# Mamba block and mixture of experts on one Trainium2 core: the step-size product on VectorE, one more buffer for the rows of B and of C, and fewer small tiles

## The chip, the cores and the metric

The kernel runs on one core of one Trainium2 chip. The metric is the device time of one execution in microseconds (us). The engines are called as in the profile: PE is TensorE (PEld its weight loads), DVE is VectorE, ACT is ScalarE, POOL is GpSimd, SP is SyncE, whose queue issues most DMAs.

## The reference

Sixteen rows (batch entries) of 512 tokens with 256 features pass through two stages. `mod` are six vectors for each row, made from `L0_c` and `L0_wmod`. In short:

```python
h = layernorm(x) * (1 + ca) + sa
x = x + ga * mamba(h)              # ga, gb: absolute value at least 0.25
h = layernorm(x) * (1 + cb) + sb
x = x + gb * experts(h)

def mamba(h):
    xb, z = split(norm(h) @ W_in)          # 512 channels each
    xb = silu(conv3(xb) + conv_b)
    dt = softplus(xb @ W_dt + b_dt)
    B, C = xb @ W_B, xb @ W_C              # 16 states
    for t in tokens:                       # A = -exp(A_log), for 512 channels and 16 states
        state = exp(dt[t] * A) * state + (dt[t] * xb[t]) * B[t]
        y[t] = sum_over_states(state * C[t])
    return h + ((y + D * xb) * silu(z)) @ W_out

def experts(h):                            # 16 experts, width 128, the best 4 of 2 groups out of 4
    return sum_e weight[t, e] * (silu(h @ gate[e]) * (h @ up[e])) @ down[e]
```

All of it is computed in float32.

## The kernel before

Everything of one row lives in SBUF with channels on the 128 partitions and the 512 tokens along them: `xb`, `gz` (the gate), `dt` and `dtx` have four blocks of 128 channels each, [128, 4, 512].

**The scan.** The work is cut into 512 steps `g`: 16 rows (a row has one slot of 32 steps), and in a row two pairs of channel blocks, each with 16 states. The states are walked up in one pair and down in the next, so that the rows of B and C used last in one pair are used first in the next. One step `g` takes, on [128, 2, 512] = 128x1024 elements:

- ACT, `decay` (L1112): two exponentials into a PSUM bank pair, `hbank[g % 2]`;
- POOL, `drive(g)` (L1335): `unit[g % 5] = dtx * B row`, run AHEAD = 2 steps before its use;
- DVE, `scan(g)` (L759): the recurrence as one tensor_tensor_scan in the PSUM bank;
- DVE, `times_c(g)` (L773): the states times the row of C, back into `unit` (the first two of a pair into `gsum`);
- POOL, `add(g - 1)` (L1347): a DMA that adds the 512 KB of `unit` to `gsum[k]`, k being g's parity; each waits until the last one of its parity has landed.

The rows of B and C are read from DRAM, broadcast over the partitions (256 KB each), by SP's queue: `load_b(g + B_LEAD)` and `load_c(g + C_LEAD)` in step g, into B_RING and C_RING buffers. `rows_held` works out which loads can be left out since the row is still in its buffer. Before, B has four buffers and a lead of 3, C three and a lead of 2.

**Step sizes.** `dtx = dt * xb` for a pair of blocks must stand before that pair's first `drive`. Before, `step_sizes` on POOL makes it (L1278: one 128x1024 product; then L1280, a memset of the two first columns of `dt` to 1e30, which cuts the scan between the two blocks). This happens 31 times; the very first product is made on DVE (`first_steps`, L837, L839).

**Beside the scan**, each engine runs the same fixed list of other stages, `streams(slot, ...)`: a stage is a generator, and its steps are spread over the moments of a slot (three to a step g; part 0, 1 and 2). ACT runs one moment behind PE, DVE two, POOL and SP three. So `step_sizes1` (second pair of the slot's row, moments 1 to 8) did its product on POOL in moment 11, step 3 of the slot, behind `drive(g + 2)`; `step_sizes0` (first pair of the coming row, moments 73 to 80) in moment 83, step 27, again behind `drive(g + 2)`.

**The experts** of the row before run at the same time, in 16 half-steps of two experts. For each: PE makes gates and ups (L504) into two of three `wbank`s; ACT the tanh of the gates into one tile, `etanh` (L1102); DVE silu (L730, `act = (etanh + 1) * gates`) and the product with the ups (L737); POOL the product with the routing weights (L1302); PE the down product (L516) into `mbank`. After the first and the second eight, DVE scales `mbank` and adds it to the result (L747, L750), and PE's next down product waits for that. `act` has two buffers.

Every engine runs its instructions in order, so one that waits holds all that stand behind it.

Of the kernel before, what the change touches and what calls it, by code (L numbers as in the profile page):

```python
# [10 lines left out]
P = 128  # L11
# [71 lines left out]
def build(nc, d, out):  # L83
# [15 lines left out]
    B_RING, C_RING, W_RING = 4, 3, 2  # L99
    B_LEAD, C_LEAD = 3, 2  # L100
# [17 lines left out]
    with ctx:  # L118
# [15 lines left out]
        half_ident = sb("half_ident", [P, P])  # L134
# [32 lines left out]
        etanh = sb("etanh", [P, 2 * HT])  # L167
        w_all = sb("w_all", [P, W_RING, 2, HT])

        sums = sb("sums", [P, TT])  # L170
        squares = sb("squares", [P, TT])
        nmean = sb("nmean", [P, TT])
        ve = sb("ve", [P, TT])
        rstd = sb("rstd", [P, TT])
        shift = sb("shift", [P, TT])
        sums2 = sb("sums2", [P, TT])
        squares2 = sb("squares2", [P, TT])
        nmean2 = sb("nmean2", [P, TT])
        ve2 = sb("ve2", [P, TT])
        rstd2 = sb("rstd2", [P, TT])  # L180
        shift2 = sb("shift2", [P, TT])
        r_th = sb("r_th", [P, TT, E])
# [6 lines left out]
        r_cut = sb("r_cut", [P, TT, E + 4])  # L189
# [3 lines left out]
        w_tok = sb("w_tok", [P, TT, E])  # L193
# [170 lines left out]
        def _(eng):  # L364
# [158 lines left out]
            def mix(row, pair):  # L523

                p = 2 * row + pair
                for a in range(2):
                    q = 2 * pair + a
                    t = fill(("y", row, q))
                    eng.matmul(t.bank[:, :], diag_d[:, q, :], xb[:, xb_at(row, q), :], start=True, stop=False)  # L529
                    for k in range(2):  # L530
                        need.wait_ge(summed[k], 16 * LATER * (p + 1))
                        m = eng.matmul(t.bank[:, :], half_ident[:, :], gsum[:, (2 * p + k) % SUMS, a, :], start=False,  # L532
                                       stop=k == 1)
                    m.then_inc(t.full, 1)
                    yield
                    yield
# [77 lines left out]
        def _(eng):  # L614
# [21 lines left out]

            def gates(row):
                for q in range(DK):
                    t = work.at["gate", row, q]
                    need.wait_ge(gate_act, DK * row + q + 1)  # L640
                    eng.scalar_tensor_tensor(out=gz[:, q, :], in0=gz[:, q, :], scalar=1.0, in1=t.bank[:, :],  # L641
                                             op0=ALU.add, op1=ALU.mult).then_inc(t.free, 1)
                    yield
                    yield

            def pick(row):
# [4 lines left out]
                bias = choice_bias[:, :].rearrange("p (a e) -> p a e", a=1).to_broadcast([P, TT, E])  # L651
                need.wait_ge(route_act, 2 * row + 2)
# [69 lines left out]
            def experts(row):  # L722
                for s in range(E + 1):
                    n = E * row + s
                    a = act[:, n % MOE_RING, :, :].rearrange("p j t -> p (j t)")
                    if s < E:

                        t = work.at["gates2", row, s]
                        need.wait_ge(etanhed, n + 1)
                        eng.scalar_tensor_tensor(out=a, in0=etanh[:, :], scalar=1.0, in1=t.bank[:, :], op0=ALU.add,  # L730
                                                 op1=ALU.mult).then_inc(t.free, 1)
# [151 lines left out]
            for m_ in range(DK):  # L883
                eng.tensor_scalar(diag_d[:, m_, :], ident[:, :], d_par[:, m_:m_ + 1], 0.5, ALU.mult,
                                  ALU.mult).then_inc(scaled_w, 1)
            eng.tensor_scalar(half_ident[:, :], ident[:, :], 0.5, None, ALU.mult).then_inc(scaled_w, 1)

            turning = turn_chunks()
            for _ in range(2 * EARLY):
                next(turning)  # L890
            stage_of = {"silu_first": lambda r: silu_inputs(r, 0),
                        "silu_last": lambda r: silu_inputs(r, 1), "gates": gates,
                        "mix0": lambda r: mix(r, 0), "mix1": lambda r: mix(r, 1),
# [26 lines left out]
        def _(eng):  # L920
# [101 lines left out]
            def gates(row):  # L1022
                for q in range(DK):
# [5 lines left out]
                    eng.activation(gz[:, q, :], t.bank[:, :], ACT.Tanh, scale=0.5).then_inc(gate_act, 1)  # L1029
# [64 lines left out]
            def experts(row):  # L1094
                for s in range(E + 1):
                    if s < E:
                        t = work.at["gates2", row, s]
                        need.wait_ge(t.full, t.after)
                        if E * row + s:
                            used = work.at["gates2", *divmod(E * row + s - 1, E)]  # L1100
                            need.wait_ge(used.free, used.after)
                        eng.activation(etanh[:, :], t.bank[:, :], ACT.Tanh, scale=0.5).then_inc(etanhed, 1)  # L1102
# [111 lines left out]
        def _(eng):  # L1214
# [54 lines left out]
            def step_sizes(row, q):  # L1269
                pair = slice(2 * q, 2 * q + 2)  # L1270
                for _ in range(8):
                    yield
                for m_ in (2 * q, 2 * q + 1):
                    t = work.at["dt", row, m_]
                    need.wait_ge(t.free, t.after)
                xb_ready(need, row)
                x0 = xb_at(row, 2 * q)
                eng.tensor_tensor(dtx[:, pair, :], dt[:, pair, :], xb[:, x0:x0 + 2, :], ALU.mult).then_inc(dtx_made, 1)  # L1278
                need.wait_ge(dtx_made, 2 * row + q + 1)
                eng.memset(dt[:, pair, 0:1], FAR).then_inc(dt_cut, 1)  # L1280
                yield

# [55 lines left out]
            def add(g):  # L1338
# [6 lines left out]
                if u >= 4:  # L1345
# [18 lines left out]
            stage_of = {"norms": norms, "step_sizes0": lambda r: step_sizes(r, 0),  # L1364
                        "step_sizes1": lambda r: step_sizes(r, 1), "stats": stats, "scale_wo": scale_wo,
                        "scale_h": scale_h}
# [232 lines left out]
```

## Time and profile before

| | before |
|---|---|
| median of 3 runs | 2733.24 us (2730.16 to 2736.14) |
| the profiled execution: its time, its span | 2725.84 us, 2724.1 us |
| granted TensorE clock, mean | 0.949 |
| PE busy | 2363.2 us, 87% |
| DVE busy | 2402.8 us, 88% |
| ACT busy | 1452.3 us, 53% |
| POOL busy | 2227.2 us, 82% |
| DMA: moved, mean rate | 596.53 MB, 219 GB/s |
| chain of work that ended last | PE 51%, POOL 14%, DVE 10%, DMA 9%, issue 9%, ACT 6% |

The profile comes from one execution that is 7.4 us quicker than the median. Busy shares are means over the span, which has a start of some 65 us without a scan and an end of some 130 us with experts alone; between them one slot follows another in about 158 us. The profile shows an instruction from its dispatch to its end, so neighbours on one engine may overlap by some tenths of a microsecond. The number in brackets behind a row of the order of time is the idle time in front of it, with what ended it; where the named releaser had long been done, it was another, often a DMA.

### The profile page before, as it was taken

How to read it: one execution, taken by the hardware profiler on the slowest of the kernel's cores; microseconds unless marked ns; L12 is line 12 of the kernel's file. 1: busy time of each engine (PE TensorE's matmuls, PEld its weight loads, DVE VectorE, ACT ScalarE, POOL GpSimd, SP SyncE). 2: the span in 40 equal slices, each digit the busy share in tenths (PEclk: the TensorE clock that was granted, in tenths of full speed). 3: DMA queues.
4: the chain of work that ended last, by engine and by line, in shares of the span. 5: the costliest groups of instructions: out<-in, count | busy, mean ns of one | idle time of the engine just before them, and what ended most of it. 6: DMA issues, size and time to landing. Idle time of an engine off the chain costs nothing.

```text
span 2724.1 us, 28747 instructions
## 1 busy us (share of the span) xinstructions
PE 2363.2 (87%) x9006; PEld 1679.9 (62%) x9006; DVE 2402.8 (88%) x2395; ACT 1452.3 (53%) x2760; POOL 2227.2 (82%) x1559
## 2 busy tenths in 40 slices
PE   6454998989999898998989899998989989898799
PEld 2222675666667566666656666675666657566678
DVE  4798999999999999999899999999999899999922
ACT  4455646565554656565465655546565554654311
POOL 2588899888889989888898888889888889987922
PEclk8676998999999999999999999999999999999999
DMA  5989898999989899999989899898989999898921
GB/s 136 248 200 247 201 251 218 241 218 234 242 218 251 216 243 222 237 239 222 238 217 235 218 233 242 213 246 221 245 215 233 239 216 247 221 234 212 247 55 51
DMA packets 338235, 596.53 MB, mean 219 GB/s; under 512 B 49680, under 2 KB 160272, under 8 KB 338080
## 3 DMA queue, kind: packets, MB, share of 16 engines
q0 software_dynamic: 72960, 243.30, 46.7%
q1 hardware_dynamic: 265120, 351.38, 41.6%
q8 instruction: 71, 1.16, 0.2%
q14 instruction: 84, 0.69, 0.1%
HBM read 349.62 MB, written 10.06 MB: 132 GB/s over the span
## 4 chain that ended last, share of the span: by engine, by line
PE 51%; POOL 14%; DVE 10%; DMA 9%; issue 9%; ACT 6%; SPq 0%; POOLq 0%; DVEq 0%; ACTq 0%
PE wbank L504 17%; PE mbank L516 9%; PE wbank L406 7%; POOL unit L1335 6%; DVE hbank L759 5%; DMA gsum<-unit 4%; PE wbank L446 4%; PE wbank L532 3%; PE wbank L394 3%; POOL act L1302 2%; POOL gsum L1347 2%; PE wbank L417 2%; PE wbank L529 2%; DMA w_all<-w_scratch 2%; ACT z L939 2%
## 5 line engine op out<-in xcount | busy, mean ns | idle before, releaser
L1335 POOL TENSOR_TENSOR unit<-dtx,b_bc 128x1024 f32<-128x1024 f32 x512 | 1353.3, 2654 | 40.7 <-DVE dtx L837 28.1
L759 DVE TENSOR_TENSOR_SCAN hbank<-hbank,unit 128x1024 f32<-128x1024 f32 x512 | 1173.1, 2291 | 83.3 <-ACT hbank L1112 78.8
L1112 ACT ACTIVATE hbank<-dt,a_neg 128x512 f32<-128x512 f32 x1024 | 668.0, 681 | 262.9 <-DVE unit L773 230.7
L516 PE MATMUL mbank<-down_t,act 128*128 128x256 f32 x2048 | 522.8, 393 | 70.9 <-POOL act L1302 50.3
L773 DVE TENSOR_TENSOR unit<-hbank,c_bc 128x1024 f32<-128x1024 f32 x448 | 546.4, 1220 | 26.1 <-DMA c_bc<-bc_scratch 2.5
L1347 POOL DMA_DIRECT2D gsum<-unit x448 | 449.3, 1003 | 126.8 <-DMA gsum<-unit 63.4
L1302 POOL TENSOR_TENSOR act<-act,w_all 128x512 f32<-128x512 f32 x256 | 363.2, 1419 | 212.1 <-DVE act L737 190.3
L504 PE MATMUL wbank<-h_t,up_t 128*128 128x256 f32 x2048 | 501.1, 389 | 10.3 <-DVE gz L641 10.3
L516 PEld LDWEIGHTS mbank<-down_t,act 128*128 128x128 f32 x2048 | 394.9, 196 | 175.7 <-POOL act L1302 69.1
L504 PE MATMUL wbank<-h_t,gate_t 128*128 128x256 f32 x2048 | 485.7, 380 | 0.0
L504 PEld LDWEIGHTS wbank<-h_t,up_t 128*128 128x128 f32 x2048 | 395.1, 195 | 107.6 <-DVE gz L641 28.8
L504 PEld LDWEIGHTS wbank<-h_t,gate_t 128*128 128x128 f32 x2048 | 386.7, 190 | 89.9 <-issue 39.0
L1102 ACT ACTIVATE etanh<-wbank 128x512 f32<-128x512 f32 x256 | 150.7, 589 | 319.5 <-PE wbank L504 319.3
L730 DVE SCALAR_TENSOR_TENSOR act<-etanh,wbank 128x512 f32<-128x512 f32 x256 | 173.9, 679 | 94.7 <-ACT etanh L1102 93.1
L406 PE MATMUL wbank<-xb,w_dt 128*128 128x512 f32 x496 | 233.1, 616 | 8.8 <-DVE xb L633 8.8
L737 DVE TENSOR_TENSOR act<-act,wbank 128x512 f32<-128x512 f32 x256 | 174.0, 680 | 18.8 <-PE wbank L504 13.5
L430 PE MATMUL wbank<-xn_t,w_in 128*128 128x512 f32 x256 | 143.1, 688 | 29.7 <-DVE gz L641 22.4
L406 PEld LDWEIGHTS wbank<-xb,w_dt 128*128 128x128 f32 x496 | 96.6, 198 | 111.8 <-issue 107.3
L532 PE MATMUL wbank<-gsum,half_ident 128*128 128x512 f32 x256 | 125.3, 610 | 27.2 <-DMA gsum<-unit 27.2
L394 PE MATMUL wbank<-xn_t,w_in 128*128 128x512 f32 x256 | 125.4, 615 | 26.4 <-DVE xb L633 22.2
L376 PE MATMUL wbank<-ident,z 128*128 128x128 f32 x256 | 42.2, 305 | 101.7 <-ACT z L939 95.1
L446 PE MATMUL wbank<-w_out,gz 128*128 128x256 f32 x512 | 121.1, 379 | 1.1 <-issue 1.1
(142 smaller groups left out, 2237.5 us busy)
## 6 DMA issues: line engine op xcount, KB each, us to landing
gsum<-unit POOLq DMA_DIRECT2D x448, 512.0 KB, 7.5
c_bc<-bc_scratch SPq DMA_DIRECT2D x464, 256.0 KB, 5.6
b_bc<-bc_scratch SPq DMA_DIRECT2D x448, 256.0 KB, 6.2
w_all<-w_scratch SPq DMA_DIRECT2D x256, 256.0 KB, 4.9
ht<-in_L_attn_x_dram SPq DMA_DIRECT2D x16, 512.0 KB, 5.2
w_out<-in_L_attn_W_out_dram SPq DMA_DIRECT2D x16, 512.0 KB, 6.4
ht<-in_L_attn_x_dram POOLq DMA_DIRECT2D x16, 512.0 KB, 8.5
out_dram<-xt SPq DMA_DIRECT2D x16, 512.0 KB, 3.3
```

The source lines that it names most:

```text
L394: m = eng.matmul(t.bank[:, :], w_in[:, k, q * P:(q + 1) * P], xn_t[:, k, :], start=k == 0, stop=k == HK - 1)
L406: m = eng.matmul(t.bank[:, :], w_dt[:, k, m_ * P:(m_ + 1) * P], xb[:, xb_at(row, k), :], start=k == 0, stop=k == DK - 1)
L446: m = eng.matmul(t.bank[:, u * H:(u + 1) * H], gz[:, k, c:c + P], w_out[:, k, :], start=k == 0, stop=False)
L504: m = eng.matmul(t.bank[:, j * HT:(j + 1) * HT], w[:, 2 * first + j, k, :], h2_t[:, row % 2, k, h * HT:(h + 1) * HT], start=k == 0, stop=k ...
L516: m = eng.matmul(mbank[:, u * H:(u + 1) * H], act[:, (n - 1) % MOE_RING, j, u * P:(u + 1) * P], down_t[:, e, :], start=(e == 0 and u == 0) ...
L532: m = eng.matmul(t.bank[:, :], half_ident[:, :], gsum[:, (2 * p + k) % SUMS, a, :], start=False, stop=k == 1)
L759: eng.tensor_tensor_scan(h, h, unit[:, g % RING, :, :].rearrange("p a t -> p (a t)"), 0.0, ALU.mult, ALU.add).then_inc(scanned, 1)
L773: eng.tensor_tensor(o, hbank[g % HB][:, :, :], c_bc[:, s:s + 1, :].to_broadcast([P, 2, T]), ALU.mult).then_inc(c_scaled, 1)
L1112: eng.activation(hbank[g % HB][:, a, :], dt[:, 2 * q + a, :], ACT.Exp, scale=a_neg[:, 2 * q + a, n:n + 1]).then_inc(decayed, 1)
L1302: eng.tensor_tensor(a, a, w_all[:, n % W_RING, :, :], ALU.mult).then_inc(weighted, 1)
L1335: eng.tensor_tensor(unit[:, g % RING, :, :], dtx[:, 2 * q:2 * q + 2, :], b_bc[:, s:s + 1, :].to_broadcast([P, 2, T]), ALU.mult).then_inc(d ...
L1347: eng.dma_start(gsum[:, (2 * p + k) % SUMS, :, :], unit[:, g % RING, :, :], accum_op=ALU.add).then_inc(summed[k], 16)
```

## The change

Five things are changed.

1. `step_sizes` moves from POOL's program to DVE's, at the same place of the plan. With DVE's lag it comes one moment earlier: `step_sizes1` in moment 10, behind `times_c` of step 3 and a product of `mix1`; `step_sizes0` in moment 82, between `times_c` of step 27 and the scan of step 28. It waits for `dt` (ACT) as before, and for the `drive`s of the row before.
2. B gets five buffers with a lead of 4, C four with a lead of 3.
3. ACT writes the experts' tanh into the `act` tile itself and DVE's silu works in place; ACT's wait for the silu before becomes a wait for the down product that last read that tile.
4. `half_ident` is gone. The factor 0.5 of the gate goes into the second half of `w_in`, scaled once at the start (a 128x1024 instruction on DVE in place of a 128x128 one).
5. Twelve statistics tiles become one, `r_cut` and `w_tok` share memory with `r_two` and `r_ch`; `pick` gets a wait for PE's last read of `w_tok`, a slot earlier.

```diff
-    B_RING, C_RING, W_RING = 4, 3, 2
-    B_LEAD, C_LEAD = 3, 2
+    B_RING, C_RING, W_RING = 5, 4, 2
+    B_LEAD, C_LEAD = 4, 3
...
-        half_ident = sb("half_ident", [P, P])
...
-        etanh = sb("etanh", [P, 2 * HT])
...
-        r_cut = sb("r_cut", [P, TT, E + 4])
+        r_cut = r_two[:, :, :].rearrange("p g k -> p (g k)")[:, 0:TT * (E + 4)].rearrange("p (t e) -> p t e", t=TT)
...
-        w_tok = sb("w_tok", [P, TT, E])
+        w_tok = r_ch
...  mix, on PE
-                        m = eng.matmul(t.bank[:, :], half_ident[:, :], gsum[:, (2 * p + k) % SUMS, a, :], start=False,
+                        m = eng.matmul(t.bank[:, :], ident[:, :], gsum[:, (2 * p + k) % SUMS, a, :], start=False,
...  on DVE
+            def step_sizes(row, q):
+                pair = slice(2 * q, 2 * q + 2)
+                for _ in range(8):
+                    yield
+                for m_ in (2 * q, 2 * q + 1):
+                    t = work.at["dt", row, m_]
+                    need.wait_ge(t.free, t.after)
+                if row:
+                    need.wait_ge(driven, (row - 1) * NU + (q + 1) * NS)
+                x0 = xb_at(row, 2 * q)
+                eng.tensor_tensor(dtx[:, pair, :], dt[:, pair, :], xb[:, x0:x0 + 2, :], ALU.mult).then_inc(dtx_made, 1)
+                need.wait_ge(dtx_made, 2 * row + q + 1)
+                eng.memset(dt[:, pair, 0:1], FAR).then_inc(dt_cut, 1)
+                yield
...  pick, on DVE
+                if row:
+                    w = work.at["w", row - 1]
+                    need.wait_ge(w.full, w.after)
...  experts, on DVE
-                        eng.scalar_tensor_tensor(out=a, in0=etanh[:, :], scalar=1.0, in1=t.bank[:, :], op0=ALU.add,
+                        eng.scalar_tensor_tensor(out=a, in0=a, scalar=1.0, in1=t.bank[:, :], op0=ALU.add,
...  at the start, on DVE
-                eng.tensor_scalar(diag_d[:, m_, :], ident[:, :], d_par[:, m_:m_ + 1], 0.5, ALU.mult,
+                eng.tensor_scalar(diag_d[:, m_, :], ident[:, :], d_par[:, m_:m_ + 1], None,
                                   ALU.mult).then_inc(scaled_w, 1)
-            eng.tensor_scalar(half_ident[:, :], ident[:, :], 0.5, None, ALU.mult).then_inc(scaled_w, 1)
+            eng.tensor_scalar(w_in[:, :, INNER:2 * INNER], w_in[:, :, INNER:2 * INNER], 0.5, None,
+                              ALU.mult).then_inc(scaled_w, 1)
...  gates, on ACT
-                    eng.activation(gz[:, q, :], t.bank[:, :], ACT.Tanh, scale=0.5).then_inc(gate_act, 1)
+                    eng.activation(gz[:, q, :], t.bank[:, :], ACT.Tanh).then_inc(gate_act, 1)
...  experts, on ACT
-                        t = work.at["gates2", row, s]
+                        n, t = E * row + s, work.at["gates2", row, s]
                         need.wait_ge(t.full, t.after)
-                        if E * row + s:
-                            used = work.at["gates2", *divmod(E * row + s - 1, E)]
-                            need.wait_ge(used.free, used.after)
-                        eng.activation(etanh[:, :], t.bank[:, :], ACT.Tanh, scale=0.5).then_inc(etanhed, 1)
+                        if n >= MOE_RING:
+                            need.wait_ge(down_done, n - MOE_RING + 1)
+                        eng.activation(act[:, n % MOE_RING, :, :].rearrange("p j t -> p (j t)"), t.bank[:, :], ACT.Tanh,
+                                       scale=0.5).then_inc(etanhed, 1)
...  on POOL
-            def step_sizes(row, q):
...
-                eng.tensor_tensor(dtx[:, pair, :], dt[:, pair, :], xb[:, x0:x0 + 2, :], ALU.mult).then_inc(dtx_made, 1)
...
-                eng.memset(dt[:, pair, 0:1], FAR).then_inc(dt_cut, 1)
```

## Rows read from the trace of the kernel before

**Rows 1.** Engines' busy times by stretch, one slot: PE, PEld, DVE, ACT, POOL, clock, DMA share, GB/s
```profile
1178.00:1336.00 158.00, 141.18 (x546) 99.59 (x545) 146.79 (x146) 88.01 (x168) 136.85 (x97) 0.98 0.92 229
```

**Rows 2.** Chain that ended last, in order of time, first slot: start, us, what
```profile
80.53 2.31 POOL dtx L1278
```

**Rows 3.** In order of time, POOL and DVE, slot 7: steps 27 and 28
```profile
1296.23 2.94 POOL L1335 TENSOR_TENSOR unit<-dtx,b_bc 128x1024 f32<-128x1024 f32 x1
1298.54 2.94 POOL L1278 TENSOR_TENSOR dtx<-dt,xb 128x1024 f32<-128x1024 f32 x1
...
1297.37 2.29 DVE L759 TENSOR_TENSOR_SCAN hbank<-hbank,unit 128x1024 f32<-128x1024 f32 x1
1300.15 0.69 DVE L730 SCALAR_TENSOR_TENSOR act<-etanh,wbank 128x512 f32<-128x512 f32 x1 [0.50 <-ACT etanh L1102]
```

**Rows 4.** Instructions of L837 and L710: ns min/median/max, first and last start
```profile
L837 DVE TENSOR_TENSOR dtx<-dt,xb x1: 1226/1226/1226, 52.9 to 52.9; 128x1024 f32<-128x1024 f32 x1
...
L710 DVE SCALAR_TENSOR_TENSOR r_w<-r_cut,r_s x16: 224/226/1749, 269.1 to 2623.6; 128x64 f32<-128x64 f32 x16
```

**Rows 5.** In order of time, POOL and DVE: L710 in slot 7, then the long one
```profile
1216.43 0.23 DVE L710 SCALAR_TENSOR_TENSOR r_w<-r_cut,r_s 128x64 f32<-128x64 f32 x1
...
1218.18 0.89 POOL L1347 DMA_DIRECT2D gsum<-unit  x1 [3.10 <-DMA gsum<-unit]
...
2491.89 3.03 POOL L1335 TENSOR_TENSOR unit<-dtx,b_bc 128x1024 f32<-128x1024 f32 x1
...
2493.27 1.75 DVE L710 SCALAR_TENSOR_TENSOR r_w<-r_cut,r_s 128x64 f32<-128x64 f32 x1
```

**Rows 6.** In order of time, DVE and POOL, slot 7: what hands work to PE
```profile
1306.75 0.69 DVE L750 TENSOR_TENSOR xt<-mbank,xt 128x512 f32<-128x512 f32 x1
1311.27 0.68 DVE L737 TENSOR_TENSOR act<-act,wbank 128x512 f32<-128x512 f32 x1
...
1287.96 1.26 POOL L1302 TENSOR_TENSOR act<-act,w_all 128x512 f32<-128x512 f32 x1 [0.43 <-DVE act L737]
```

**Rows 7.** In order of time, PE, its two pauses behind step 28, slot 7
```profile
1307.59 1.97 PE L516 MATMUL mbank<-down_t,act 128*128 128x256 f32 x8 [1.19 <-DVE xt L750]
...
1316.09 1.13 PE L516 MATMUL mbank<-down_t,act 128*128 128x256 f32 x4 [3.09 <-POOL act L1302]
1317.06 5.29 PE L406 MATMUL wbank<-xb,w_dt 128*128 128x512 f32 x8
...
1324.78 3.60 PE L406 MATMUL wbank<-xb,w_dt 128*128 128x512 f32 x8
```

**Rows 8.** The same, PE, slots 1 and 14, first and last of the 14
```profile
366.63 1.13 PE L516 MATMUL mbank<-down_t,act 128*128 128x256 f32 x4 [1.48 <-POOL act L1302]
...
2432.27 1.13 PE L516 MATMUL mbank<-down_t,act 128*128 128x256 f32 x4 [2.14 <-POOL act L1302]
2433.24 5.29 PE L406 MATMUL wbank<-xb,w_dt 128*128 128x512 f32 x8
```

**Rows 9.** Engines' busy times by stretch: PE, PEld, DVE, ACT, POOL, granted clock, DMA share
```profile
1318.00:1320.00 2.00, 2.00 (x3) 0.67 (x2) 1.90 (x3) 0.12 (x1) 1.24 (x1) 0.50 0.87 216
```

**Rows 10.** In order of time, POOL and DVE, slot 8: steps 3 and 4
```profile
1335.05 2.63 POOL L1335 TENSOR_TENSOR unit<-dtx,b_bc 128x1024 f32<-128x1024 f32 x1
...
1336.80 0.69 DVE L730 SCALAR_TENSOR_TENSOR act<-etanh,wbank 128x512 f32<-128x512 f32 x1 [0.71 <-ACT etanh L1102]
1338.06 2.30 DVE L759 TENSOR_TENSOR_SCAN hbank<-hbank,unit 128x1024 f32<-128x1024 f32 x1 [0.57 <-ACT hbank L1112]
```

**Rows 11.** Who waited for whom: us in total, times, longest us
```profile
POOL act L1302 <- DMA w_all<-w_scratch: 19.3, 9, 9.6
POOL unit L1335 <- DMA b_bc<-bc_scratch: 9.5, 7, 3.2
```

**Rows 12.** DMA issues: count, KB each, median us to landing
```profile
c_bc<-bc_scratch SPq DMA_DIRECT2D x464, 256.0 KB, 5.6
```

**Rows 13.** In order of time, DVE at the start: four 128x128 scalings
```profile
54.21 7.24 DVE L884 TENSOR_SCALAR diag_d<-ident,d_par 128x128 f32<-128x128 f32 x4
```

More of the change, by code:

```diff
@@ L166, in build @@
         act = sb("act", [P, MOE_RING, 2, HT])
-        etanh = sb("etanh", [P, 2 * HT])
         w_all = sb("w_all", [P, W_RING, 2, HT])
[L170 to L182, printed above, removed]
+        stat = sb("stat", [P, 12, TT])
+        sums, squares, nmean, ve, rstd, shift, sums2, squares2, nmean2, ve2, rstd2, shift2 = (
+            stat[:, k, :] for k in range(12))
         r_s = sb("r_s", [P, TT, E])
@@ L892, in _ @@
                         "silu_last": lambda r: silu_inputs(r, 1), "gates": gates,
+                        "step_sizes0": lambda r: step_sizes(r, 0), "step_sizes1": lambda r: step_sizes(r, 1),
                         "mix0": lambda r: mix(r, 0), "mix1": lambda r: mix(r, 1),
@@ L1267, in norms @@
                 yield
-            def step_sizes(row, q):
[L1270 to L1277, printed above, removed]
-                eng.tensor_tensor(dtx[:, pair, :], dt[:, pair, :], xb[:, x0:x0 + 2, :], ALU.mult).then_inc(dtx_made, 1)
-                need.wait_ge(dtx_made, 2 * row + q + 1)
-                eng.memset(dt[:, pair, 0:1], FAR).then_inc(dt_cut, 1)
-                yield
             def stats(row):
@@ L1362, in _ @@
             need.wait_ge(consts, 7)
-            stage_of = {"norms": norms, "step_sizes0": lambda r: step_sizes(r, 0),
-                        "step_sizes1": lambda r: step_sizes(r, 1), "stats": stats, "scale_wo": scale_wo,
-                        "scale_h": scale_h}
+            stage_of = {"norms": norms, "stats": stats, "scale_wo": scale_wo, "scale_h": scale_h}
             first_norm()
```

## The prediction

> **What bounds the kernel now.** I read the busy times of one slot first. Slots repeat every 158 us, and in one of them PE is busy 141 us, DVE 147, POOL 137, and the DMA engines 0.92 of the time [rows 1]. Nothing has much room, so the busy shares don't say who sets the time. The chain of waits does: it passes from engine to engine, and three questions matter. Where is POOL's product L1278 on it? Where would DVE's new instruction stand on it? Who is waiting just behind that place?
>
> L1278 itself stands on the chain once in 31 times, in the first slot [rows 2]. So its removal from POOL is worth little by itself.
>
> The new instruction has two places. The first is step 27, between `times_c(27)` and `scan(28)`. There DVE goes on at 1297.37 without a pause, has one pause of 0.50 us at 1300.15, in front of L730 [rows 3], and then none until L750 and L737, which end at 1307.44 and 1311.95 [rows 6]. Both are awaited by PE: after L750 by 0.15 us, with a pause of 1.19 us in front, and after L737 by way of POOL's L1302 (1.26 us), with a pause of 3.09 us [rows 6, 7]. Behind this PE goes from product to product. So from step 28 to step 31 the chain is DVE's, and all that is put ahead of it arrives at PE less 0.50 us. The second place is step 3: there DVE has pauses of 0.71 and 0.57 us right behind [rows 10], since ACT's tanh waits for PE. There PE sets the time.
>
> **Part 1: the product on DVE.** On DVE the same instruction took 1.226 us; the memset of two columns, with its wait for the product, lies between 0 and the 0.225 of L710 with its 64 elements [rows 4], and I put it at 0.10. That is 31 times 1.33, 41 us, if nothing else happens. But something else can happen: this instruction reads two SBUF tensors (`dt`, `xb`). Another DVE instruction that does so is L710. Fifteen of 16 took some 0.225 us; one took 1.75 [rows 4]. The fifteen ran while POOL ran no product, as the one of slot 7, in a pause of POOL of 3.10 us. The long one began at 2493.27, when a `drive` of POOL was running that ended at 2494.92, and it ended at 2495.02 [rows 5], 0.10 us behind. DVE waited until POOL had finished. The start shows the same with another kind of instruction: four scalings of 128x128 took 7.24 us together, beside three `drive`s [rows 13].
>
> So every L710 that met a product of POOL was held, but that is one. The Trainium skill, SBUF — State Buffer, section "SBUF: two separate sides", says that VectorE and GpSimd share a pair of ports as an exclusive lock, held for a whole instruction, and that a VectorE instruction with two SBUF inputs takes it against a GpSimd one that reads SBUF. Perfetto Trace Analysis (Optimizing Scalar/DVE Operations) warns for that reason that moving work between these two "might not help". By that rule the new product waits each time that it meets a `drive`, which makes the 3.0 us below; taken as an accident, the long L710 would leave 1.25 us there, and the sum would be that of the first rival.
>
> I take the blocking, since the one event agrees with it and none speaks against it.
>
> Then at step 27: a `drive` is running when DVE arrives at 1297.37; it ends at 1296.23 + 2.94 = 1299.17 [rows 3]. The product ends 1.226 - 0.225 + 0.10 = 1.10 us later, at 1300.27, and with the memset `scan(28)` starts at 1300.4, 3.0 us late. Less the pause of 0.50, everything up to L737 is 2.5 us late. It is so in each slot 1 to 14 (DVE and POOL stand to each other as here in all of them, to 0.2 us); slot 0 has no experts, slot 15 no product here.
>
> What arrives at PE: the first pause grows from 1.19 to 3.7 us. PE then comes to its second one at 1316.09 - 3.09 + 2.5 = 1315.5; L737 ends at 1314.45 and L1302 at 1315.7. So PE goes on some 0.25 us behind its arrival in place of G, the second pause of today: the shift of a slot is 2.75 - G. G is 1.48 in slot 1, 2.14 in slot 14 [rows 8], 3.09 in slot 7, and 1.8 in the mean of the 14, the shortest being 1.2. That gives 0.95 x 14 = +13 us. That G shrinks is POOL's gain: without L1278, which occupied it until 1301.48 [rows 3], its `add`s go out up to 2.3 us earlier and no longer hold L1302.
>
> **PE's clock.** Behind the pause of 3.09 us in slot 7 the granted clock was 0.50 for a stretch [rows 9], the lower level of 1.2 GHz, and the eight matmuls of L406 took 5.29 us in place of 3.60 [rows 7], 1.7 more. Behind 2.14 us in slot 14 it was the same [rows 8]. Three of the 14 slots show it here (7, 8, 14), the other eleven don't, with pauses of 1.2 to 2.4 us. A first pause of 3.7 us in each slot is longer than any of these, so I expect the low clock behind most of them: a slot with it shifts by 2.5 + 1.7 - G = 2.4, 34 us in all 14, less 5 for the three of today: +29. Between +13 (no new one) and +29 I take three quarters of the way, +25. Bounds: +8 (none, and today's three gone) to +29.
>
> **At step 3** a `drive` ends at 1337.68, so the product ends at 1338.78 and L730 starts at 1338.9 in place of 1336.80; the scan at 1338.06 is 1.4 us late after the two pauses. What hides it is PE, busy without a pause for the next 20 us, with ACT behind it. Taken at 0; if that cover is gone, 16 x 1.4 = +23 us. Below 0 it can't be: POOL's time there is no one's wait.
>
> **Part 2: buffers for B and C.** At the turn of a slot's two pairs the last rows of the first pair are reused: five and four in place of four and three. By `rows_held`, C's loads fall from 464 to 448 [rows 12] and B's by 16 too, so two of 256 KB less in a slot. And SP leaves them out just when it stores the routing weights and reads the first `w_all`, which L1302 awaits: 19.3 us in 9 waits, 9.6 of it one; the rows of B were awaited for 9.5 us [rows 11]. At best all but the 9.6 goes, -19; at worst nothing, as POOL or DVE are next at those places within 0.4 us in slot 7. Nothing speaks for a loss: a load still waits for the step before last's reader, and SP's queue is held no longer. I take -7.
>
> **Parts 3 to 5.** Nothing. ACT's tanh waits only for PE today, and PE's gates come behind the down product that frees the tile. The in-place silu has one SBUF input like before. The wait in `pick` was over a slot earlier. At the start, scaling half of `w_in` is the last instruction ahead of DVE's first turned weights: 0.4 us more than `half_ident`, or 2.4 if a `drive` blocks it as the ones before [rows 13]; against this stand up to 2.3 us that the chain of the first slot loses with L1278 [rows 2]. I take 0, with -2 to +2.
>
> **The sum:** +25 + 0 - 7 + 0 = +18 us: 2744 for the profiled execution of 2725.84, which was 7 us under the median, and 2733 + 18 = **2751 us** for the median.
>
> **Rivals.**
> - *Not held, and faster.* If the long L710 is an accident, or if the relieved POOL runs no `drive` when DVE arrives, DVE is late by 1.33 - 0.08 overlap - 0.50 = 0.75 us only, at the same place. PE's shift is 0.75 + 0.25 - G = -0.8, times 14 -11 us; the first pause stays under 2 us, the three low clocks go (-5), and the loads give -7: -23, 2710 us. It decides when DVE's delay is under G - 0.25, 1.5 us. For it: POOL loses 2.9 us of work at each place, so its schedule may move. Against it: the long L710 [rows 5], and that POOL has nothing new between steps 4 and 26 to move it. 0.22.
> - *Balance.* Blocked, but the clock stays high behind the longer pause (+8), and the loads give more (-8): about 2733 us. 0.17.
> - *DVE is late everywhere.* The delay of step 3 isn't hidden either: +18 + 23 = 2774 us. For it: DVE has but 11 us of pauses in a slot of 158 [rows 1]. Against it: PE's unbroken run there. 0.08. And in the extreme no pause takes up anything: 15 x 3.0 + 16 x 2.7 = 88 us, with the loads 2814 us. 0.07.
> - *The forecast*, 2739 to 2765 us: 0.46.
>
> **Range and chances.** 2706 to 2776 us leaves out the extreme and the lower half of the fast rival's spread. Both signs hold much of the chance; the likeliest case's own range is 2739 to 2765. A measurement of this kernel can tell some 0.2%, 5.5 us, from no change. Faster 0.24 (the first rival and a little of the balance), same 0.16 (the rest of it and an edge of the forecast), slower 0.60.
>
> **What would show it.** The new DVE product: about 2.9 us at step 27 and 2.7 at step 3 if held, 1.23 if not. PE's pause in front of L516 behind L750: 3.7 us against 1.9. The clock in the stretch behind it: 0.5 or 1. PE's second pause: short in both. The scan of step 28: 3.0 us behind `times_c(27)`. L1302's waits for `w_all`: shorter. The forecast is wrong if the product is short, or if PE's lateness at step 31 is made up by a pause later in the slot that I took for fixed.

## The result and the profile after

The changed kernel takes 2759.72 us (median of 4 runs, 2757.09 to 2765.98), the kernel before, beside it, 2731.7 (2726.53 to 2736.14): 1.0113 times the time, 95% interval 1.0089 to 1.0137. It is slower by 28 us between the medians (31 by the ratio), where 18 were forecast, and the time lies inside the range.

| | after |
|---|---|
| the profiled execution: its time, its span | 2761.49 us, 2759.8 us |
| granted TensorE clock, mean | 0.938 |
| DMA: moved, mean rate | 588.13 MB, 213 GB/s |

The profiled executions are 35.7 us apart: that of before was some 6 us under its median, that of after 2 us above. First the busy times, then the chain that ended last:

```profile
PE 2380.3 (86%) x9006; PEld 1698.5 (62%) x9006; DVE 2491.7 (90%) x2457; ACT 1452.2 (53%) x2760; POOL 2154.5 (78%) x1497
```

```profile
PE 34%; DVE 28%; issue 14%; POOL 13%; ACT 7%; DMA 4%; SPq 0%; DVEq 0%; POOLq 0%
```

DVE is 89 us busier, which is 31 times 2.87, and its share of the chain goes from 10 to 28%. POOL is 73 us less busy, though its product had been on the chain only once. Next the engines' busy times in one slot (PE, PEld, DVE, ACT, POOL, clock, DMA share, GB/s), which answers [rows 1]:

```profile
1208.00:1366.00 158.00, 142.62 (x547) 102.22 (x546) 151.05 (x151) 88.28 (x169) 132.50 (x93) 0.97 0.90 225
```

And the moved product by its durations (minimum, median, maximum in ns, first and last start):

```profile
L635 DVE TENSOR_TENSOR dtx<-dt,xb x31: 2751/2887/5065, 86.2 to 2489.3; 128x1024 f32<-128x1024 f32 x31
```

None of the 31 took the 1.226 us of its free form [rows 4]: each met a `drive` and ended 1.09 us behind the end of one. In order of time in slot 7, POOL and DVE, steps 27 and 28 (answers [rows 3]):

```profile
1327.35 2.93 POOL L1329 TENSOR_TENSOR unit<-dtx,b_bc 128x1024 f32<-128x1024 f32 x1
...
1328.48 2.89 DVE L635 TENSOR_TENSOR dtx<-dt,xb 128x1024 f32<-128x1024 f32 x1
1331.43 0.06 DVE L637 MEMSET dt<- 128x2 f32 x1
1331.48 2.30 DVE L765 TENSOR_TENSOR_SCAN hbank<-hbank,unit 128x1024 f32<-128x1024 f32 x1
```

The `drive` ends at 1330.28, the product at 1331.37, 1.09 us behind, and the scan starts 3.0 us after DVE could have started it. What PE gets of that (answers [rows 7]):

```profile
1341.10 2.73 PE L504 MATMUL mbank<-down_t,act 128*128 128x256 f32 x8 [3.59 <-DVE xt L756]
1343.62 2.85 PE L492 MATMUL wbank<-h_t,gate_t 128*128 128x256 f32 x8
1346.31 1.89 PE L492 MATMUL wbank<-h_t,up_t 128*128 128x256 f32 x8
1348.04 1.03 PE L504 MATMUL mbank<-down_t,act 128*128 128x256 f32 x4
1348.90 3.60 PE L394 MATMUL wbank<-xb,w_dt 128*128 128x512 f32 x8
```

The first pause is 3.6 us (1.19 before), the second is gone, and the eight down products and the eight gates behind the pause take 2.73 and 2.85 us against 1.97 and 1.89 at full clock. The granted clock there, in slots 1, 7 and 14 (columns as above):

```profile
376.20:379.20 3.00, 3.00 (x7) 2.45 (x8) 3.00 (x3) 0.00 (x0) 2.75 (x2) 0.50 1.05 254
...
1341.50:1344.50 3.00, 3.00 (x11) 2.39 (x10) 3.00 (x3) 0.00 (x0) 2.34 (x1) 0.61 0.99 252
...
2464.50:2467.50 3.00, 3.00 (x10) 2.47 (x9) 3.00 (x3) 0.00 (x0) 2.44 (x2) 0.61 1.05 271
```

In all of the slots 1 to 14 the clock is 0.50 to 0.68 in such a stretch. Before, it never fell behind the first pause, and behind the second one in three of the 14. The waits over the whole span (us in total, times, longest), the first two lines of before, then of after (POOL's two answer [rows 11]):

```profile
PE mbank L516 <- DVE xt L750: 20.6, 15, 3.9
...
PE mbank L516 <- POOL act L1302: 50.3, 35, 4.0
```

```profile
PE mbank L504 <- DVE xt L756: 51.7, 15, 3.6
...
PE mbank L504 <- POOL act L1296: 13.1, 12, 3.5
...
POOL act L1296 <- DMA w_all<-w_scratch: 9.4, 1, 9.4
POOL unit L1329 <- DMA b_bc<-bc_scratch: 0.2, 1, 0.2
```

PE waits 31 us more for DVE and 37 less for POOL, so the waits alone don't explain the loss. The whole account of steps 28 to 31, from the rows of slots 1 to 14, is this, in the mean of a slot: the first pause is 2.4 us longer and the second, 1.8 us, is gone; the products of PE between the first pause and the first of L394 (before, of L406) take 7.9 us in place of 6.4 at the lower clock; and the eight of L394 take 0.4 less than those of L406, since the three low stretches of before are gone. Together that is +1.7 us, 24 us in 14 slots.

**Where the time lies.** The starts of the 512 scans cut a span into parts: up to the first scan, slot 0, slots 1 to 14 in first halves (steps 0 to 15, with the place of step 3) and second halves (with that of step 27), slot 15 up to the end of its last scan, the end. What step 27 does can reach into steps 0 to 2 of the next slot, and so into a first half. In us, one profiled execution each:

| kernel | start | slot 0 | 1–14, first halves | 1–14, second halves | slot 15 | end |
|---|---|---|---|---|---|---|
| before | 64.9 | 149.5 | 1110.4 | 1108.3 | 151.0 | 140.0 |
| after | 69.4 | 156.9 | 1114.7 | 1131.6 | 147.1 | 140.0 |
| only_steps | 65.3 | 154.7 | 1108.6 | 1144.9 | 148.8 | 141.2 |
| rings_back | 63.9 | 155.5 | 1113.2 | 1144.4 | 149.1 | 139.9 |
| both_pool | 68.1 | 150.6 | 1112.1 | 1106.6 | 146.5 | 142.2 |
| first_pair_pool | 68.2 | 153.6 | 1113.0 | 1103.3 | 148.0 | 139.9 |
| second_pair_pool | 67.6 | 149.7 | 1111.8 | 1135.2 | 148.4 | 144.2 |
| ahead_sbuf | 66.3 | 153.4 | 1124.9 | 1157.1 | 146.6 | 142.0 |
| ahead_psum | 67.0 | 149.3 | 1088.9 | 1113.5 | 146.0 | 140.0 |
| early_scalings | 59.5 | 154.3 | 1112.3 | 1130.0 | 146.9 | 142.7 |
| both_pool_early | 60.9 | 148.9 | 1113.1 | 1103.8 | 147.6 | 141.3 |
| dt_from_psum | 60.4 | 149.8 | 1098.1 | 1113.5 | 146.2 | 142.2 |

After against before: start +4.5, slot 0 +7.4, slots 1 to 14 +27.6 (23.3 of it in second halves), slot 15 -3.9. A part moves by a few us from one execution to another, and a profiled execution may lie some us beside its kernel's median (before 6 under, `both_pool` 2 above, `early_scalings` 7 under). So the verdicts below rest on the ratios, and the parts say where.

### The profile page after: what moved, and what is told of

It reads as the page before. It is cut to its first block, busy times and chain, and to the rows that moved or that the text cites. A ratio compares the mean times of both kernels' runs of the same rounds, so it can differ in the third digit from the quotient of the medians.

```text
span 2759.8 us, 28724 instructions
## 1 busy us (share of the span) xinstructions
PE 2380.3 (86%) x9006; PEld 1698.5 (62%) x9006; DVE 2491.7 (90%) x2457; ACT 1452.2 (53%) x2760; POOL 2154.5 (78%) x1497
## 2 busy tenths in 40 slices
DMA packets 333626, 588.13 MB, mean 213 GB/s; under 512 B 49168, under 2 KB 159760, under 8 KB 333472
## 4 chain that ended last, share of the span: by engine, by line
PE 34%; DVE 28%; issue 14%; POOL 13%; ACT 7%; DMA 4%; SPq 0%; DVEq 0%; POOLq 0%
DVE hbank L765 14%; PE wbank L492 9%; PE mbank L504 6%; POOL unit L1329 5%; DVE unit L779 4%; PE wbank L434 4%; PE wbank L394 3%; PE wbank L520 3%; PE wbank L382 2%; DMA gsum<-unit 2%; POOL gsum L1341 2%; DVE dtx L635 2%; PE wbank L454 2%; ACT z L947 2%; POOL stat L1233 2%
## 5 line engine op out<-in xcount | busy, mean ns | idle before, releaser
L1296 POOL TENSOR_TENSOR act<-act,w_all 128x512 f32<-128x512 f32 x256 | 348.3, 1361 | 333.2 <-DVE act L743 323.8
L504 PE MATMUL mbank<-down_t,act 128*128 128x256 f32 x2048 | 533.1, 399 | 65.3 <-DVE xt L756 51.7
L504 PEld LDWEIGHTS mbank<-down_t,act 128*128 128x128 f32 x2048 | 401.2, 199 | 165.6 <-issue 90.5
L492 PE MATMUL wbank<-h_t,up_t 128*128 128x256 f32 x2048 | 491.0, 383 | 10.3 <-DVE gz L644 10.3
L492 PE MATMUL wbank<-h_t,gate_t 128*128 128x256 f32 x2048 | 498.6, 387 | 0.9 <-DVE act L736 0.9
L492 PEld LDWEIGHTS wbank<-h_t,gate_t 128*128 128x128 f32 x2048 | 398.0, 195 | 96.6 <-issue 39.0
L492 PEld LDWEIGHTS wbank<-h_t,up_t 128*128 128x128 f32 x2048 | 388.0, 191 | 105.3 <-DVE gz L644 28.8
L1109 ACT ACTIVATE act<-wbank 128x512 f32<-128x512 f32 x256 | 150.7, 589 | 300.3 <-PE wbank L492 300.1
L736 DVE SCALAR_TENSOR_TENSOR act<-act,wbank 128x512 f32<-128x512 f32 x256 | 173.6, 678 | 71.7 <-ACT act L1109 69.6
L394 PE MATMUL wbank<-xb,w_dt 128*128 128x512 f32 x496 | 227.1, 602 | 8.8 <-DVE xb L621 8.8
L394 PEld LDWEIGHTS wbank<-xb,w_dt 128*128 128x128 f32 x496 | 94.5, 193 | 107.8 <-issue 103.4
L520 PE MATMUL wbank<-gsum,ident 128*128 128x512 f32 x256 | 124.4, 606 | 27.9 <-DMA gsum<-unit 27.9
```

The lines of the kernel that those rows point to most:

```text
L394: m = eng.matmul(t.bank[:, :], w_dt[:, k, m_ * P:(m_ + 1) * P], xb[:, xb_at(row, k), :], start=k == 0, stop=k == DK - 1)
L492: m = eng.matmul(t.bank[:, j * HT:(j + 1) * HT], w[:, 2 * first + j, k, :], h2_t[:, row % 2, k, h * HT:(h + 1) * HT], start=k == 0, stop=k ...
L504: m = eng.matmul(mbank[:, u * H:(u + 1) * H], act[:, (n - 1) % MOE_RING, j, u * P:(u + 1) * P], down_t[:, e, :], start=(e == 0 and u == 0) ...
L520: m = eng.matmul(t.bank[:, :], ident[:, :], gsum[:, (2 * p + k) % SUMS, a, :], start=False, stop=k == 1)
L1296: eng.tensor_tensor(a, a, w_all[:, n % W_RING, :, :], ALU.mult).then_inc(weighted, 1)
```

## The experiments

The theory: the product costs at step 27 of a slot, because a `drive` holds it there and PE waits behind. Rivals: the place of step 3 costs too; POOL's new schedule or the buffers cost; the 1.3 us of DVE's own work would cost the same without any holding. Each ratio is against executions of the kernel before that ran beside that group of kernels; their medians were 2733.0 us for the first four kernels, 2728.9 for the next four, 2727.4 for the last two.

**The product alone.** The kernel before, with nothing but `step_sizes` moved.

```diff
 on DVE, before's rings and tiles
+            def step_sizes(row, q):
...
 on POOL
-            def step_sizes(row, q):
...
```

> The kernel before with the product of step_sizes on DVE and nothing else of the change. Theory (DVE is held by POOL's drive at step 27, the other parts give some 7 us back and cost 4.5 at the start): 2731.7 + 28 + 7 - 4.5 = 2762 us, products of 2.8 to 2.9 us, PE's pause behind L750's line 3.6 us. Rival 'other parts' (buffers, in-place tanh or the start make the loss): 2732 to 2737 us. Rival 'DVE's work' (its 41 us of new work count wherever they stand, held or not): also some 2760, so this run doesn't tell it from the theory.

Measured: 2764.8 us, 1.0105 (1.0069 to 1.0142), +29 to +32 us. The product's durations, and PE's wait for DVE:

```profile
L647 DVE TENSOR_TENSOR dtx<-dt,xb x31: 2751/2886/6108, 80.7 to 2490.1; 128x1024 f32<-128x1024 f32 x31
```

```profile
PE mbank L516 <- DVE xt L765: 51.6, 14, 4.7
```

The move alone gives the whole loss, with the same held product and PE's same wait. Its cost lies in the second halves, +36.6 us; the first halves don't grow. One of the 31 took 6.1 us, and PE's pause behind it was 4.7.

**The two places apart.** The changed kernel with both products back on POOL, with only that of step 27 back (`first_pair_pool`), and with only that of step 3 back (`second_pair_pool`).

```diff
 stages of DVE: both_pool drops both entries, the others one
-                        "step_sizes0": lambda r: step_sizes(r, 0), "step_sizes1": lambda r: step_sizes(r, 1),
...
 stages of POOL
+                        "step_sizes0": lambda r: step_sizes(r, 0), "step_sizes1": lambda r: step_sizes(r, 1)}
```

> The kernel after with both products back on POOL; the buffers, the in-place tanh and the scaling of w_in stay. Theory: the gain of the buffers (-7) against the longer start (+4.5): 2729 us, 2724 to 2734. Rival 'other parts': 2750 or more.

Measured: 2725.7 us, 0.9975 (0.9958 to 0.9992). All the other parts of the change together gain 7 us (2 to 11).

> The kernel after with the product of the coming row's first pair (step 27) back on POOL, the one of step 3 still on DVE. Theory (step 3's is hidden by PE, but for some 4 us in the first two slots): 2733 us, 2728 to 2738. Rival 'DVE's work' (half of the work, half of the loss): 2745 us.

Measured: 2732.0 us, 0.9994 (0.9978 to 1.0010).

> The kernel after with the product of step 3 back on POOL, the one of step 27 still on DVE. Theory: nearly all of the loss stays, 2755 us, with PE's pause of 3.6 us and the low clock behind it in slots 1 to 14. Rival 'DVE's work': 2745 us.

Measured: 2757.1 us, 1.0071 (1.0043 to 1.0099). The product's durations, in `first_pair_pool` and in `second_pair_pool`:

```profile
L635 DVE TENSOR_TENSOR dtx<-dt,xb x16: 2752/2762/6107, 84.0 to 2454.9; 128x1024 f32<-128x1024 f32 x16
```

```profile
L635 DVE TENSOR_TENSOR dtx<-dt,xb x15: 1687/2881/2994, 201.3 to 2443.3; 128x1024 f32<-128x1024 f32 x15
```

PE's wait for DVE, in the same order, with `both_pool` ahead of them:

```profile
PE mbank L504 <- DVE xt L756: 19.7, 15, 3.0
```

```profile
PE mbank L504 <- DVE xt L756: 18.1, 15, 1.4
```

```profile
PE mbank L504 <- DVE xt L756: 50.4, 14, 3.7
```

In both kernels the product is held. At step 3, 16 times 2.76 us on DVE leave PE's wait where it was and cost 6 us in all, 3.0 of it in slot 0 and 1.5 in slot 15: in slots 1 to 14 nothing is lost, as forecast (the scan of step 4 comes 1.5 us later in the mean, that of step 12 no longer does). At step 27 it costs 31 us against `both_pool`, 28.3 of them in slots 1 to 14. The rival "DVE's work" asked for 2745 us in both kernels; they lie 25 us apart.

**Holding or work?** The same place, once with the lock and once without. In both kernels the product of DVE stands between the scan and `times_c` of steps 3 and 27. In `ahead_sbuf` it is the product itself. In `ahead_psum` one operand is the scan's PSUM bank, times zero, plus `dt`: `dtx` then lacks the factor `xb`, which this kernel leaves out.

```diff
 on DVE, both: called between scan(g) and times_c(g)
-                for _ in range(8):
-                    yield
+                need.wait_ge(scanned, g + 1)
...
 ahead_psum alone
-                eng.tensor_tensor(dtx[:, pair, :], dt[:, pair, :], xb[:, x0:x0 + 2, :], ALU.mult).then_inc(dtx_made, 1)
+                eng.scalar_tensor_tensor(
+                    out=dtx[:, pair, :].rearrange("p a t -> p (a t)"),
+                    in0=hbank[g % HB][:, :, :].rearrange("p a t -> p (a t)"), scalar=0.0,
+                    in1=dt[:, pair, :].rearrange("p a t -> p (a t)"), op0=ALU.mult, op1=ALU.add).then_inc(dtx_made, 1)
```

> The kernel after with DVE's products one place earlier: between scan and times_c of steps 3 and 27. It is the control of the next run. Theory: still held by the drive (it starts 0.6 us later at step 27, so the product would have to wait up to 4 us): 2760 to 2772 us. Rival 'DVE's work': 2760.

Measured: 2789.1 us, 1.0220 (1.0183 to 1.0256).

> The same as the control, but the product reads the states' PSUM bank in place of xb (it computes 0 times the bank plus dt, so dtx lacks the factor xb): one SBUF input in place of two, and the same DVE work. Theory (two SBUF inputs are what holds it): products of 1.22 us, PE's pause behind L756's line under 2.5 us, no low clock behind it in most slots, 2715 us, 2708 to 2725. Rival 'DVE's work': the same as the control, within 5 us.

Measured: 2706.5 us, 0.9928 (0.9902 to 0.9953), just under the range expected. The product's durations, first in `ahead_sbuf`, then in `ahead_psum`:

```profile
L634 DVE TENSOR_TENSOR dtx<-dt,xb x31: 1367/3178/4116, 80.1 to 2516.6; 128x1024 f32<-128x1024 f32 x31
```

```profile
L634 DVE SCALAR_TENSOR_TENSOR dtx<-hbank,dt x31: 1224/1225/1227, 80.9 to 2433.3; 128x1024 f32<-128x1024 f32 x31
```

POOL and DVE in order of time at step 27 of slot 7, in the same order of kernels:

```profile
1332.56 2.92 POOL L1330 TENSOR_TENSOR unit<-dtx,b_bc 128x1024 f32<-128x1024 f32 x1
...
1332.48 4.09 DVE L634 TENSOR_TENSOR dtx<-dt,xb 128x1024 f32<-128x1024 f32 x1
```

```profile
1294.18 2.94 POOL L1333 TENSOR_TENSOR unit<-dtx,b_bc 128x1024 f32<-128x1024 f32 x1
...
1294.11 1.23 DVE L634 SCALAR_TENSOR_TENSOR dtx<-hbank,dt 128x1024 f32<-128x1024 f32 x1
```

And PE's wait for DVE:

```profile
PE mbank L504 <- DVE xt L754: 65.3, 14, 5.0
```

```profile
PE mbank L504 <- DVE xt L757: 25.2, 14, 2.1
```

At step 27 both meet a `drive` that starts within 0.1 us of them. (At step 3 of slots 2 to 15 the product of `ahead_sbuf` meets only the end of one and takes 1.37 us.) With two operands in SBUF the product takes until 1.1 us behind the `drive`'s end; with one in PSUM it takes 1.23 us beside it. The same number of DVE instructions over the same elements at the same places: 83 us apart, and the one that isn't held is faster than the kernel before. So it is the holding, not the work. `ahead_sbuf` was dearer than expected. Against the changed kernel its pause of PE grows from 3.6 to 4.64 us, 14.6 us over 14 slots. Of the other 21 us in slots 1 to 14, some 15 are the clock's: behind the longer pause it stays low for longer (in slot 7 granted 0.50 and 0.54 in two stretches of 3 us from 0.4 us behind the pause on, 0.61 and 0.82 in the changed kernel). PE in `ahead_sbuf`, slot 7, the same products as in the changed kernel above:

```profile
1347.36 3.75 PE L504 MATMUL mbank<-down_t,act 128*128 128x256 f32 x8 [4.64 <-DVE xt L754]
1350.90 3.19 PE L492 MATMUL wbank<-h_t,gate_t 128*128 128x256 f32 x8
```

They take 3.75 and 3.19 us, where the changed kernel has 2.73 and 2.85; in the mean of the 14 slots PE is 1.1 us longer from the first pause to L394. The last 6 us have no shown cause.

**The buffers.** The changed kernel with the rings and leads of before.

```diff
-    B_RING, C_RING, W_RING = 5, 4, 2
-    B_LEAD, C_LEAD = 4, 3
+    B_RING, C_RING, W_RING = 4, 3, 2
+    B_LEAD, C_LEAD = 3, 2
```

> The kernel after with four and three buffers for B and C and leads of 3 and 2, as before. Theory: loses the buffers' 7 us and gains up to 4.5 at the start, where the fourth row of B lets a drive hold the scaling of w_in: 2762 us, 2757 to 2768. If the buffers are worth nothing: 2755 us.

Measured: 2767.1 us, 1.0150 (1.0123 to 1.0178). That is 0.0037 above the changed kernel's ratio, 10 us, and the two intervals overlap, so it may be anything from nothing to 20. By the parts it is -11.4 us in slots 1 to 14 and -2 in slot 15 for the larger rings, against +5.5 at the start. Two products of `rings_back` took 6.1 us, with pauses of PE of 4.7 behind them, and none of the changed kernel at step 27 did; that is part of the 11.4, and whether the rings are its reason isn't shown. What happens there, DVE and POOL in order of time, first `rings_back`, then the changed kernel (answers [rows 13]):

```profile
52.73 7.25 DVE L890 TENSOR_SCALAR diag_d<-ident,d_par 128x128 f32<-128x128 f32 x4
59.90 0.68 DVE L892 TENSOR_SCALAR w_in<-w_in 128x1024 f32<-128x1024 f32 x1
...
61.88 4.66 POOL L1329 TENSOR_TENSOR unit<-dtx,b_bc 128x1024 f32<-128x1024 f32 x2 [2.18 <-DMA b_bc<-bc_scratch]
```

```profile
54.02 9.35 DVE L890 TENSOR_SCALAR diag_d<-ident,d_par 128x128 f32<-128x128 f32 x4
63.28 2.84 DVE L892 TENSOR_SCALAR w_in<-w_in 128x1024 f32<-128x1024 f32 x1
...
54.04 11.54 POOL L1329 TENSOR_TENSOR unit<-dtx,b_bc 128x1024 f32<-128x1024 f32 x5 [29.17 <-DVE dtx L843]
```

With three rows of B ahead POOL stops for 2.18 us, and DVE's last scaling runs free. With four, five `drive`s run back to back, and the five scalings wait behind them: 12.2 us in place of 7.9, ahead of the first scan. Each that is held takes 2.4 to 2.8 us. The fourth of `diag_d` is held in all the kernels with the larger rings and this order of the start, that of `w_in` only in this execution: in the profiled executions of `both_pool`, `first_pair_pool`, `second_pair_pool`, `ahead_sbuf` and `ahead_psum` it took 0.68 us. So some 2.1 us of the start are the rings' steady price, and the rest isn't.

**The scalings first.** The five scalings of DVE (and the small one of `choice_bias`) before `first_steps`, with the product on DVE (`early_scalings`) and on POOL (`both_pool_early`).

```diff
-            first_steps()
...  behind the scalings
+            first_steps()
```

> The kernel after with DVE's scalings at the start (choice_bias, diag_d, half of w_in) ahead of the very first product instead of behind it, where DVE waits 8.3 us for ACT and POOL runs no drive. Theory: the five scalings take under 2 us in place of 12, the first scan starts some 10 us earlier if nothing else holds it; the bank for ACT and PE may, so 2750 us, 2748 to 2756. If the start is set by something else: 2760.

Measured: 2754.4 us, 1.0099 (1.0070 to 1.0129).

> Both products on POOL, the buffers of after, and the five scalings at the start ahead of the first product. Theory: the 2725.7 of both_pool less the 5 to 6 us that the order of the start gave in early_scalings: 2720 us, 0.4% under the kernel before.

Measured: 2715.6 us, 0.9957 (0.9942 to 0.9972). The first scan starts 9.9 and 7.2 us earlier, so those scalings were on the path: ahead of the first product, with no `drive` beside them, the five take 1.8 us together. The ratios gain 0.0014 and 0.0018, 4 and 5 us, within their intervals, so that the gain in the whole time isn't shown; where the rest went wasn't settled.

**A version with the factor in PSUM.** ACT makes the softplus in its PSUM bank and copies it to `dt`; DVE multiplies the bank by `xb`, one block of 128x512 at a time and some steps earlier in the plan; the scalings come first. Nothing is left out.

```diff
 on ACT
-                    eng.activation(dt[:, m_, :], t.bank[:, :], ACT.Softplus, bias=b_dt[:, m_:m_ + 1]).then_inc(t.free, 1)
+                        eng.activation(t.bank[:, :], t.bank[:, :], ACT.Softplus, bias=b_dt[:, m_:m_ + 1]).then_inc(dt_act, 1)
...
+                        eng.activation(dt[:, m_, :], t.bank[:, :], ACT.Identity).then_inc(dt_act, 1)
 on DVE
-                eng.tensor_tensor(dtx[:, pair, :], dt[:, pair, :], xb[:, x0:x0 + 2, :], ALU.mult).then_inc(dtx_made, 1)
+                    eng.tensor_tensor(dtx[:, m_, :], t.bank[:, :], xb[:, xb_at(row, m_), :], ALU.mult).then_inc(t.free, 1)
```

> A full version whose product on DVE isn't held: ACT's softplus stays in its PSUM bank, ACT copies it into dt, and DVE multiplies the bank by xb, block by block (0.68 us each), early enough for the bank; with the start of early_scalings. Theory: the 2706.5 of ahead_psum, less 5 us for the start, plus a few us for 1.36 in place of 1.22 us on DVE and the bank that is held longer: 2704 us, 2698 to 2715. Rival (DVE's or ACT's additional work, or the bank, sets the time): 2730 or more.

Measured: 2707.5 us, 0.9931 (0.9906 to 0.9957), faster than both kernels. The products' durations, and PE's wait for DVE:

```profile
L635 DVE TENSOR_TENSOR dtx<-wbank,xb x62: 673/681/682, 67.5 to 2434.6; 128x512 f32<-128x512 f32 x62
```

```profile
PE mbank L504 <- DVE xt L757: 25.1, 14, 1.8
```

All 62 take 0.67 to 0.68 us, whatever POOL does, 42 us in place of 92, and PE's first pause is 1.79 us. The fair comparison for the move alone is `both_pool_early`, which has the same buffers and the same start and leaves the product on POOL: 2715.6 us beside it. So taking this product from POOL gains 8 us (some 3 to 12 by the spread of the runs), if the product doesn't read two SBUF tensors; the rest of the 0.7% comes from the buffers and the order of the start.

## Why the prediction was right, and where it was off

- **The product is held.** Right, and the step that carried the forecast: 2.89 us at step 27 (forecast 2.9) and 2.76 at step 3 (2.7). One long L710 [rows 5] told it, which was thin ground; `ahead_psum` shows that this, and not the work, is what costs.
- **DVE's delay arrives at PE.** Right: a first pause of 3.6 us where 3.7 was forecast, in each of 14 slots, and a second, behind POOL's L1302 (now L1296), that is gone there [rows 7, 8].
- **The clock.** Right in kind. I took three quarters of the way to the low clock in every slot, which made +25, and it was low in 14 of 14, whose full price I had put at +29. The rows give +24 for steps 28 to 31: the products behind the pause lost 0.76 and 0.96 us in slot 7, as the eight L406 of [rows 7] had, but by the start of L394 only 1.5 us of that were left in the mean. So the frequency was taken too low and the price of a slot too high, and that the two cancel is luck. The other 3.5 of the 27.6 us lie in first halves. `second_pair_pool` against `both_pool` gives +28.3. With the rings of before the second halves lost more, 36 us, above my upper bound of 29.
- **Step 3.** Right in slots 1 to 14: `first_pair_pool` shows no loss there. Taken at 0 for all 16 it was wrong in slot 0, which has no experts. "Below 0 it can't be" isn't shown: with unheld products the first halves of `ahead_psum` are 23 us shorter than those of `both_pool`. Some 14 of these are there before the product of step 3 is made and so come from step 27; the rest may be what POOL's relief at step 3 is worth, and no kernel has that place alone.
- **Slot 0.** This is the missing term. I noted that no experts run there and then gave it nothing; without them PE has, I take it, no work to hide DVE's delay behind. `first_pair_pool` and `second_pair_pool` show that the growth is that of step 3's product: 3.0 us with it, none without. The slot grew by 7.4 us, and is 153.4 to 156.9 us in all six kernels whose product of step 3 stands on DVE with two SBUF inputs, 148.9 to 150.6 in the others. The products there took 4.15 and 3.51 us, and that of step 3 in slot 1 took 5.07; the one of 4.15 and the one of 5.07 lost to a `drive` that started after them.
- **The start.** 0 was forecast, with -2 to +2; it was +4.5. The 2.4 us for a blocked `w_in` was weighed as the worse end and came true in this execution (2.84 against 0.68), not in five other kernels with the same start. The four scalings ahead of it grew as well, in all of them, from 7.24 to 9.35, because part 2 feeds POOL at the start. I had costed the buffers only at the turn of the pairs.
- **Buffers.** -7 (0 to -19) was forecast. The waits went as described, b_bc from 9.5 to 0.2 us and w_all from 19.3 to the one of 9.4, C's loads from 464 to 448. In slots 1 to 14 they gave 11 us against `rings_back`, and the start took 5.5 back. In `both_pool` those slots are as long as before (2218.7 and 2218.8 us), but its profiled execution lay 2 us above the median and that of before 6 under, so a gain of the buffers with the product on POOL isn't excluded; by the ratios all other parts gain 7 us.
- **The sum.** In the profiled executions +36 against +18: slots 1 to 14 27.6 against 18, slot 0 and the start 12 against 0, slot 15 -3.9 against nothing. In the medians it was +28; some 8 of the 36 are the distance of the two profiled executions from their medians.
- **The fast rival.** Its condition, a product that isn't held, was wrong here, but its price was near: -23 us, where `ahead_psum`, whose product isn't held, has -20 (0.9928), at a slightly earlier place.

The Trainium skill, SBUF — State Buffer, section "SBUF: two separate sides", says of the pair that whichever instruction starts first gets it. The traces agree that a product with two SBUF inputs is held (2.89 us in the median), and that one PSUM input frees it (1.225). On who wins they don't fit in each case: products of 5.07 and 6.1 us had been dispatched before the first `drive` ended, and yet the next `drive` went ahead of them (last section).

## What to carry to other kernels

Before an elementwise step moves from GpSimd to VectorE, count its SBUF inputs and look at what GpSimd runs at the new place: with two SBUF inputs beside a stream of GpSimd products it waited here for the rest of the other's instruction, 2.9 us in place of 1.2, and what it costs in the end is decided by who waits behind it. Making one operand come from PSUM turned the same move, with the same order of the start, from +1.0% (`early_scalings`) to -0.7%; with the product left on GpSimd it was -0.4%. And a deeper ring for one engine can lengthen what another does at the start, since it takes away the pauses in which the other ran free.

## What the runs showed of the hardware that was not expected

In the seven kernels with this product on DVE and both inputs in SBUF, each of its 186 instances ends 1.08 to 1.09 us behind the end of a `drive`, whether it took 1.37 us or 6.1. And a held product can lose to a `drive` that starts after it, by more than 0.1 us too. DVE and POOL of the changed kernel in order of time, in slots 0 and 1:

```profile
86.25 4.15 DVE L635 TENSOR_TENSOR dtx<-dt,xb 128x1024 f32<-128x1024 f32 x1
...
86.67 2.64 POOL L1329 TENSOR_TENSOR unit<-dtx,b_bc 128x1024 f32<-128x1024 f32 x1
```

```profile
239.31 2.65 POOL L1329 TENSOR_TENSOR unit<-dtx,b_bc 128x1024 f32<-128x1024 f32 x1
...
241.19 5.07 DVE L635 TENSOR_TENSOR dtx<-dt,xb 128x1024 f32<-128x1024 f32 x1
...
242.22 2.95 POOL L1329 TENSOR_TENSOR unit<-dtx,b_bc 128x1024 f32<-128x1024 f32 x1
```

The first pair: the `drive` starts 0.42 us after the product and ends at 89.31, the product at 90.40, 1.09 behind. The second: the product starts beside one `drive`, and ends at 246.26, 1.09 us behind the next one, which started 1.03 us after it. When the first one ended, at 241.96, the product had been waiting for 0.8 us, and the next one's row begins only 0.26 us later. Four products took 6.1 us in this way: one in `only_steps`, one in `first_pair_pool`, two in `rings_back`. The one of `first_pair_pool`:

```profile
236.61 2.65 POOL L1343 TENSOR_TENSOR unit<-dtx,b_bc 128x1024 f32<-128x1024 f32 x1
...
237.43 6.11 DVE L635 TENSOR_TENSOR dtx<-dt,xb 128x1024 f32<-128x1024 f32 x1
...
239.51 2.94 POOL L1343 TENSOR_TENSOR unit<-dtx,b_bc 128x1024 f32<-128x1024 f32 x1
```

It was dispatched 2.08 us before the second `drive` and ended 1.09 behind it. Rows show an instruction from its dispatch, so where two start within some tenths of a microsecond the true order can't be told from them; here a waiting product let a later one by. What decides it stays open.
